# Units of two independently placed 128-row blocks in a routed feed-forward stage

## The reference

```
x = x + tanh(g_xattn) * xattn(layernorm(x), ctx)
logits = layernorm(x) @ gate_w          # 4096 tokens x 8 experts
topv, topi = top_k(logits, 2);  w = softmax(topv)
u = h @ Wu[e];  v = h @ Wv[e];  s = silu(u) * v;  Y = s @ Wo[e]     # 512 -> 128 -> 512
x = x + tanh(g_ffn) * sum over the two chosen experts of w * Y
```

## Time and profile before

| | us |
|---|---|
| median of 3 runs (lowest, highest) | 1020.25 (1018.52, 1021.1) |
| the profiled execution, its own time | 1017.04 |
| its span | 1015.3 |
| TensorE busy | 882.5 |
| VectorE busy | 689.9 |
| ScalarE busy | 568.1 |
| GpSimd busy | 530.5 |
| mean granted TensorE clock | 0.96 |

### The profile page before, as it was taken

The page is one execution under the profiler, slowest core; times in us unless marked ns, Lnnn a source line. Parts: engine busy times, 40 slices in busy tenths (PEclk is TensorE's granted clock), DMA queues, the critical chain, the costliest instruction groups (busy, mean ns, idle before and its releaser), DMA issues. The chain is left out here.

```text
span 1015.3 us, 22868 instructions
## 1 busy us (share of the span) xinstructions
PE 882.5 (87%) x8250; PEld 536.1 (53%) x8250; DVE 689.9 (68%) x1612; ACT 568.1 (56%) x1022; POOL 530.5 (52%) x643
## 2 busy tenths in 40 slices
PE   4878999999999999999999999997670899899990
PEld 2334555555555555555555555554340678677770
DVE  5577987677877887787787688688466455345540
ACT  4367766567546656755666665566430466456550
POOL 6222253454466456546545654547754155667765
PEclk9999999999999999999999999999885899999995
DMA  7557834645652354355245433753423589899997
GB/s 264 144 152 225 266 119 123 187 118 116 162 158 73 102 166 109 79 157 164 64 118 151 111 77 95 246 180 95 151 95 136 157 183 206 169 215 213 221 170 100
DMA packets 120509, 153.21 MB, mean 151 GB/s; under 512 B 42960, under 2 KB 75728, under 8 KB 119632
## 3 DMA queue, kind: packets, MB, share of 16 engines
q1 hardware_dynamic: 96624, 101.77, 35.2%
q0 software_dynamic: 16864, 37.40, 18.8%
q10 hardware_dynamic: 6912, 12.59, 4.1%
HBM read 67.06 MB, written 56.56 MB: 122 GB/s over the span
## 5 line engine op out<-in xcount | busy, mean ns | idle before, releaser
L700 POOL TENSOR_TENSOR Pl<-P,Ph 128x512 f16<-128x512 f32 x128 | 152.6, 1203 | 167.5 <-ACT Ph L786 167.0
L783 ACT ACTIVATE P<-ST 128x512 f32<-128x512 f32 x256 | 154.5, 603 | 128.9 <-PE ST L1476 109.2
L984 DVE TENSOR_REDUCE mx<-MX 128x1 f32<-128x512 f32 x256 | 168.7, 685 | 27.9 <-PE MX L1461 27.6
L786 ACT ACTIVATE Ph<-ST 128x512 f16<-128x512 f32 x256 | 155.7, 608 | 1.2 <-remote 0.7
L750 POOL DMA_INDIRECT out_dram<-V,Ph x78 | 121.9, 1563 | 62.2 <-ACT V L938 43.7
L1678 PE MATMUL MX<-heads,tiles 128*128 128x256 f16 x936 | 116.8, 276 | 5.7 <-DVE heads L1359 5.4
L1488 PE MATMUL PV<-V,Ph 128*128 128x65 f16 x1024 | 112.0, 194 | 9.8 <-issue 9.6
L1490 PE MATMUL PV<-V,Ph 128*128 128x64 f16 x1024 | 112.2, 195 | 1.8 <-issue 1.8
L1492 PE MATMUL PV<-V,Pl 128*128 128x65 f16 x1024 | 111.8, 193 | 0.7 <-issue 0.6
L1488 PEld LDWEIGHTS PV<-V,Ph 128*128 128x128 f16 x1024 | 96.4, 97 | 29.8 <-issue 11.8
L1490 PEld LDWEIGHTS PV<-V,Ph 128*128 128x128 f16 x1024 | 95.9, 98 | 19.1 <-issue 1.8
(11 more groups left out here) (261 smaller groups left out, 1880.1 us busy)
## 6 DMA issues: line engine op xcount, KB each, us to landing
heads<-expert_rows SPq DMA_DIRECT2D x39, 516.0 KB
heads<-q_hi SPq DMA_DIRECT2D x124, 64.0 KB, 2.5
heads<-k_hi SPq DMA_DIRECT2D x124, 64.0 KB, 2.9
second_norm<-in_x_dram SPq DMA_DIRECT2D x28, 256.0 KB, 3.1
out_dram<-second_norm SPq DMA_DIRECT2D x28, 256.0 KB, 2.2
tiles<-in_x_dram ACTq DMA_DIRECT2D x24, 256.0 KB, 3.1
tiles<-in_ctx_dram ACTq DMA_DIRECT2D x24, 256.0 KB, 3.9
expert_rows<-zero_rows SPq DMA_DIRECT2D x8, 516.0 KB, 5.6
```

What stands on the lines that cost most here:

```text
L700: nc.gpsimd.tensor_tensor(Pl[:, hh, c, :], P32[:, c, :], Ph[:, hh, c, :], ALU.subtract).then_inc(pl_pool, 1)
L783: nc.scalar.activation(P32[:, c, :], ST[:, c % 2, :], ACT.Exp, scale=0.125 / SC2).then_inc(p_ready, 1)
L786: nc.scalar.activation(Ph[:, hh, c, :], ST[:, c % 2, :], ACT.Exp, scale=0.125 / SC2).then_inc(ph_ready, 1)
L984: nc.vector.tensor_reduce(out=mx[:, k // TT, k % TT:k % TT + 1], in_=MX[:, (k + odd) % 2, :], axis=AXX, op=ALU.max).then_inc(mx_taken, 1)
```

## The change

A unit is now two blocks of 128 list rows, and each block (a "window") has its own expert, its own first row and its own flags. Lists are rounded up to multiples of 128: `WINDOWS = 64 + 8 = 72`, `UNITS = 36`.

- SyncE reads two offsets and issues two row loads per unit, one row to a partition in each.
- TensorE reads two experts per unit; `up` runs the 12 products once for each window, on 128 columns; `down` takes each window's weights.
- VectorE's table runs over 72 windows; the last window of a list now comes fourth; two bounds (`EARLY = (3, 4)`); flags between windows 1, 2 and 3 apart (`shared`).
- GpSimd issues the two adds one by one, each behind a count from the table and a `hold`. In the first two units the second add waits for the first.
- Blank prefixes and outsiders: half as many rows, 4 and 8 DMAs where there were 8 and 16.
- Scale selection (`unit_weights`) has one more small instruction.

```diff
-    UR = 2 * P
-    REGION = UR + ROWS
-    UNITS = ROWS * K // UR + E - 1
+    UR = K * P
+    REGION = P + ROWS
+    WINDOWS = ROWS * K // P + E
+    UNITS = WINDOWS // K
-    EARLY = 3
+    EARLY = (3, 4)
...
-                first = sp.value_load(unit_off[0:1, s:s + 1], min_val=0, max_val=E * REGION - UR)
-                sp.dma_start(xg_words[:, r], table[bass.ds(first, UR), :].rearrange("(p k) c -> p k c", k=K)) \
-                    .then_inc(rows_ld[r], 16)
+                for k in range(K):
+                    w = s * K + k
+                    first = sp.value_load(unit_off[0:1, w:w + 1], min_val=0, max_val=E * REGION - P)
+                    sp.dma_start(xg_words[:, r, k], table[bass.ds(first, P), :]).then_inc(rows_ld[r], 16)
...
-                for t in range(K):
-                    nc.gpsimd.indirect_dma_start(table.rearrange("r (q w) -> (r q) w", w=4),
-                                                 bass.IndirectOffsetOnAxis(out_pos[:, t, e:e + 1], 0),
-                                                 out_head[:, t, :].bitcast(U32), None).then_inc(outsider_st, 16)
+                nc.gpsimd.indirect_dma_start(table.rearrange("r (q w) -> (r q) w", w=4),
+                                             bass.IndirectOffsetOnAxis(out_pos[:, e:e + 1], 0),
+                                             out_head[:].bitcast(U32), None).then_inc(outsider_st, 16)
...
                 hold()
-                pool.wait_ge(y_taken, K * (s + 1))
+                pool.wait_ge(y_taken, K * s + 1)
                 since(pool, added[s % 2], s // 2 * 2 * 16)
-                for k in range(K):
-                    nc.gpsimd.indirect_dma_start(out_rows, bass.IndirectOffsetOnAxis(ids[:, s, k:k + 1], 0),
-                                                 y_sb[:, s % YR, k, :], None, compute_op=ALU.add) \
-                        .then_inc(added[s % 2], 16)
+                add(s, 0)
+                if s < 2:
+                    pool.wait_ge(added[s % 2], 16)
+                else:
+                    first = pool.value_load(need[1][0:1, s:s + 1], min_val=2 * 16, max_val=32 * UNITS)
+                    pool.wait_ge(added[s % 2], first)
+                hold()
+                pool.wait_ge(y_taken, K * s + 2)
+                add(s, 1)
...
+                for k in range(len(EARLY)):
+                    link(nc.vector.tensor_tensor(ucmp2, ucmp, spread_e(nt[:, 2 + k, :]), ALU.mult))
+                    link(nc.vector.tensor_reduce(before, ucmp2, AXX, ALU.add))
+                    nc.vector.tensor_tensor(late[k], limit, before, ALU.is_ge)
+                    link(nc.vector.scalar_tensor_tensor(out=early[k], in0=limit, scalar=float(P), in1=before,
+                                                        op0=ALU.add, op1=ALU.is_le))
+
+                def shared(dst, d):
+
+                    here, there = slice(d, WINDOWS), slice(0, WINDOWS - d)
+                    dst, apart, differ = dst[:, here], other[:, here], flag[:, here]
+                    nc.vector.tensor_tensor(differ, ue[:, here], ue[:, there], ALU.not_equal)
+                    nc.vector.tensor_tensor(apart, late[0][:, there], early[0][:, here], ALU.mult)
+                    link(nc.vector.tensor_tensor(dst, late[1][:, there], early[1][:, here], ALU.mult))
+                    link(nc.vector.tensor_tensor(apart, apart, dst, ALU.max))
+                    link(nc.vector.tensor_tensor(dst, off[:, here], off[:, there], ALU.subtract))
+                    nc.vector.scalar_tensor_tensor(out=differ, in0=apart, scalar=0.5, in1=differ, op0=ALU.is_lt, op1=ALU.mult)
+                    link(nc.vector.tensor_tensor(dst, dst, dst, ALU.mult))
+                    link(nc.vector.scalar_tensor_tensor(out=dst, in0=dst, scalar=float(P * P), in1=differ,
+                                                        op0=ALU.is_lt, op1=ALU.max))
...
-                for k, (m, a, c) in enumerate(parts):
-                    w = FW[n][m][:, bass.ds(e, 1), c * P:(c + 1) * P].rearrange("p o n -> p (o n)")
-                    last = nc.tensor.matmul(dst, w, uT[:, s % 2, a, c * UR:(c + 1) * UR], start=k == 0,
-                                            stop=k == len(parts) - 1)
+                for t in range(K):
+                    for k, (m, a, c) in enumerate(parts):
+                        w = FW[n][m][:, bass.ds(e[t], 1), c * P:(c + 1) * P].rearrange("p o n -> p (o n)")
+                        last = nc.tensor.matmul(dst[:, t * P:(t + 1) * P], w,
+                                                uT[:, s % 2, a, c * UR + t * P:c * UR + (t + 1) * P], start=k == 0,
+                                                stop=k == len(parts) - 1)
...
-                        w = FW["o"][m][:, bass.ds(e, 1), :].rearrange("p o n -> p (o n)")
+                        w = FW["o"][m][:, bass.ds(e[t], 1), :].rearrange("p o n -> p (o n)")
...
-            def expert_of(s):
-                return pe.value_load(unit_expert[0:1, s:s + 1], min_val=0, max_val=E - 1)
+            def experts_of(s):
+                return [pe.value_load(unit_expert[0:1, w:w + 1], min_val=0, max_val=E - 1)
+                        for w in range(K * s, K * s + K)]
```

More of the change, by code:

```diff
@@ L1142, in unit_table @@
             def unit_table():
-                spread_e = lambda z: z.unsqueeze(1).to_broadcast([P, UNITS, E])
-                spread_u = lambda z: z.unsqueeze(2).to_broadcast([P, UNITS, E])
-                before, block_, limit, off, over, blocks, flag, bound, early = (uw[:, k, :] for k in range(9))
+                spread_e = lambda z: z.unsqueeze(1).to_broadcast([P, WINDOWS, E])
+                spread_u = lambda z: z.unsqueeze(2).to_broadcast([P, WINDOWS, E])
+                before, block_, limit, off, over, blocks, flag, other = (uw[:, k, :] for k in range(8))
@@ L1151, in unit_table @@
+                late, early = ([uw[:, 8 + 2 * i + k, :] for k in range(2)] for i in range(2))
                 link(nc.vector.tensor_tensor(nt[:, 0, :], base[:], C["start"][:], ALU.subtract))
-                nc.vector.tensor_scalar(nt[:, 1, :], nt[:, 0, :], float(-UR), None, ALU.add)
-                nc.vector.tensor_tensor(nt[:, 2, :], early_base[:], C["start"][:], ALU.subtract)
+                nc.vector.tensor_scalar(nt[:, 1, :], nt[:, 0, :], float(-P), None, ALU.add)
+                for k in range(len(EARLY)):
+                    nc.vector.tensor_tensor(nt[:, 2 + k, :], early_base[:, k, :], C["start"][:], ALU.subtract)
@@ L1174, in unit_table @@
                 link(nc.vector.tensor_tensor(ucmp2, ucmp, spread_e(nt[:, 1, :]), ALU.mult))
-                link(nc.vector.scalar_tensor_tensor(out=blocks, in0=blocks, scalar=-2.0, in1=flag,
+                link(nc.vector.scalar_tensor_tensor(out=blocks, in0=blocks, scalar=-4.0, in1=flag,
                                                     op0=ALU.add, op1=ALU.mult))
@@ L1195, in unit_table @@
-                link(nc.vector.tensor_reduce(bound, ucmp2, AXX, ALU.add))
-                link(nc.vector.scalar_tensor_tensor(out=early, in0=limit, scalar=float(UR), in1=bound,
-                                                    op0=ALU.add, op1=ALU.is_le))
-                link(nc.vector.tensor_tensor(bound, limit, bound, ALU.is_ge))
-                link(nc.vector.tensor_tensor(bound[:, 0:UNITS - 1], bound[:, 0:UNITS - 1], early[:, 1:UNITS], ALU.mult))
-                link(nc.vector.tensor_tensor(before[:, 0:UNITS - 1], ue[:, 1:UNITS], ue[:, 0:UNITS - 1], ALU.not_equal))
@@ L1206, in unit_table @@
-                link(nc.vector.tensor_tensor(step_, step_, before[:, 0:UNITS - 1], ALU.max))
-                nc.vector.scalar_tensor_tensor(out=need[:, 1:UNITS], in0=step_, scalar=32.0, in1=C["need"][:, 0:UNITS - 1],
-                                               op0=ALU.mult, op1=ALU.add).then_inc(need_ready, 1)
+                nc.vector.tensor_tensor(valid.rearrange("p u k -> p (u k)"), C["row_no"][:].to_broadcast([P, WINDOWS]),
+                                        block_, ALU.is_ge)
+                for k in range(len(EARLY)):
+                    link(nc.vector.tensor_tensor(ucmp2, ucmp, spread_e(nt[:, 2 + k, :]), ALU.mult))
[3 more added lines that the diff above has]
+                                                        op0=ALU.add, op1=ALU.is_le))
@@ new lines, in unit_table @@
+                one, two, three = before, block_, blocks
+                for d, dst in ((1, one), (2, two), (3, three)):
+                    shared(dst, d)
+                of = lambda z, k: z.rearrange("p (u k) -> p u k", k=K)[:, 1:UNITS, k:k + 1].rearrange("p u o -> p (u o)")
+                flags = other[:, 0:UNITS - 1], other[:, UNITS:2 * UNITS - 1]
+                nc.vector.tensor_tensor(flags[0], of(one, 0), of(two, 0), ALU.max)
+                link(nc.vector.tensor_tensor(flags[1], of(two, 1), of(three, 1), ALU.max))
@@ new lines, in unit_table @@
+                link(nc.vector.tensor_tensor(flags[0], flags[0], flags[1], ALU.max))
```

(7 more changed lines are left out.)

126 lines of the change are left out of this document (58 added, 68 removed).

## The result

The kernel after takes 1049.34 us, median of 4 runs (1048.35 to 1052.79), against 1020.1 (1018.52 to 1021.1) for the kernel before on the same chip: ratio 1.0294, 95% interval 1.0267 to 1.0321. It is slower by 29 us, as forecast (1049, range 1030 to 1067).

What follows compares the result with a forecast made beforehand. The prediction took TensorE's array (4.81 us a unit) as the bound, then its sequencer (6.5) after the change. Span 796.2 + 234 + 1 + 3 + 10.2 = 1044.4; median 1020.25 + 29 = 1049 us, range 1030 to 1067.

Steps and rivals of the forecast that it cites:

- The mechanism: Units' stage: the change makes TensorE's sequencer the bound, 6.5 us a unit against 4.87 for the array.
- The first rival (the sequencer does not bind): Units' stage: sequencer steps shrink or run beside the issue, about 5.3 us a unit, 1006 us; chance 0.11.
- The pace of the sequencer: TensorE's sequencer, per unit: addresses 4.46 us, two expert readings 1.60, waits and transposes 0.4; sum 6.5 us.
- 36 x 0.124: TensorE's sequencer, per unit: 36 register instructions where there were 18, at 0.124 us each, 4.46 us.
- The array busy about three quarters: TensorE's array in the units' stage: a sign of the prediction being right, idle a quarter of the time.
- Attention: "nothing, at most a microsecond of gain": GpSimd in attention: 8 outsiders' DMAs of 1.02 us less and half the blank rows gain nothing, at most a microsecond.
- The table: VectorE before the first unit: a longer table puts the first up-matmul at 796.2 instead of 792.69, 3.5 us.
- The end: From TensorE's end to GpSimd's last add: 3 us, before 13.9; then 10.2 us to the span's end stay.
- GpSimd and DMA: Units' stage: GpSimd busy some 5 us a unit, costing nothing; row loads in 2064-byte packets 4.9 to 6.5, nearer 4.9.
- The clock: TensorE in the units' stage: expected at 1.00; the rival, half clock, 104 us more, 1153 us, chance 0.04.
- The sum: Whole span: start 796.2, units 234, half clock 1, end 3 and 10.2: 1044.4, which is 29.1 over 1015.3.

Runs made afterwards that it cites:

- c_two: Kernel before with the change's TensorE code: two expert readings, `up` in 128-column halves, own addresses for each half, `down` too; ratio 1.0602.
- l_down: Kernel after with `down` taking the first window's expert for both, 34 addresses a unit instead of 36; 1043.64 us, ratio 1.0227 to the kernel before.
- m_onev: Kernel after with v computed with the first window's expert for both windows, 28 addresses a unit; 1020.39 us, ratio 0.9995 to the kernel before.
- l_third: Kernel after with a third, unused expert reading per unit on TensorE; 1070.81 us, ratio 1.0492 to the kernel before.
- h_wide: Kernel after with TensorE's part as before: one expert reading, `up` on 256 columns, `down` with one expert; ratio 0.9899 to the kernel before.
- c_split: Kernel before with each up-matmul of 256 columns cut in two of 128, both halves with the same expert and addresses; ratio 1.0018.
- e_outs: Kernel before with 8 outsiders' DMAs instead of 16; ratio 0.9970.
- g_even: Kernel before with all 16 outsiders' DMAs, two in the first and third step of each batch of four (before: first and second); ratio 1.0002.

## Why the prediction held, and where it did not

**The mechanism** held. c_two shows it alone: two expert registers, with their readings and their addresses and everything else as before, make the kernel slower, and l_down, m_onev and l_third show that addresses and readings each count. The first rival (the sequencer does not bind) and its 5.3 us a unit is what h_wide measures, and the kernel after is not there.

**The pace of the sequencer** was 6.5 us a unit, and is 6.71. From the starts of TensorE's sequencer instructions over 27 units: 36 addresses at 0.132 us are 4.76 (forecast 36 x 0.124 = 4.46); two readings 1.54 (forecast 1.60); three waits 0.42 (forecast 0.4): 6.72. The step that was mis-sized is "36 x 0.124": 0.124 is the median, and some 12% of the steps take 0.15 to 0.31. I used the mean for the loads and the median for the steps.

**The array busy about three quarters** failed as a sign, though its cause held: the rows show 213.07 of 243 us. A matmul's row is 0.22 us long and the next may start 0.06 after it, so gaps of up to 0.16 us don't show. c_split shows 40.00 of 40.00 with a unit in 4.87, this kernel 35 of 40 with one in 6.7: a busy share says little of pace where short matmuls are handed over one by one. The better sign was the same 24 matmuls taking 1.50 us from the queue and 2.21 at the sequencer's pace.

**Attention: "nothing, at most a microsecond of gain"** is the step that failed. It was 4.3 us between the two traces. One pair of traces is a weak measure of it, since the same attention of the kernel after reaches the table's first large operation between 770.40 and 775.40 us in four traces (after, l_down, l_third, m_onev); the medians of e_outs give 3.8 us for the same DMAs. I took GpSimd's idle time as slack for every placement of its work; its products collide with VectorE's in four steps.

**The table** took 2.7 us more from its first large operation to the first up-matmul (21.06 against 18.32), and 0.3 ahead of it: 3.0, forecast 3.5. Part of that is an addition: 4 x 0.78, 20 x 0.27 and 13 x 0.13 are 10.2 us and not 10.8, which would have made the forecast 2.9.

**The end** was costed at 3 us from TensorE's end to the last add, and took 4.7 (1033.0 to 1037.74): the second add of the unit before last still had to go out ahead of the last two, at 1.95 us each.

**GpSimd and DMA** held. The first adds wait for one another (804.08, 810.30, 815.93, 821.20, 827.02) and no stall reaches TensorE; `hold` waits 22.4 us for landings in the whole stage: twice at the start (809.85, 820.86) and for three flagged units (865.87, 880.28, 947.14), as many as the lists had said. Row loads between 841 and 861:

```profile
q1 hardware_dynamic: 867, 1.59, 24.9%
```

That is 15.7% per MB against 14.4: packets of half the size cost a tenth more per byte, near the end that was taken and far from double.

**The clock** held: 1.00 from 794.8 to 1037, with TensorE idle for 0.46 to 1.08 us ahead of nearly every up u. The Trainium skill, page "TensorE: Matmul & The Clock Gate", section "A second HAM failure mode: psum-queue depth-cycling", tells of another kernel in which frequent micro-idles between matmul groups made the clock oscillate. Here they did not.

**The sum**: start 4.7 us early (attention 4.3, table 0.4), units 6.5 late, end 1.7 late, so the span came out 3.5 above its 1044.4. That the median met 1049 to half a microsecond is luck: errors of 4.7, 6.5 and 1.7 us nearly cancel, and the 3.5 that is left was made good because the profiled execution of before was 3.2 below its median and that of after was not.

Not tried: pairing the windows so that all units but the few at the lists' ends have one expert and one set of addresses. It might reach toward h_wide's 0.9899 with the whole computation, but needs another table and other flags.

## What to carry to other kernels

Where matmuls take their weights by a register, count the different addresses that the engine's sequencer works out (0.13 us each here) and the register readings (0.77 each), and compare the sum with the array's time: two registers where there was one doubled it here, and matmuls of half the width did not matter. Idle time of GpSimd is slack only where its operations don't meet those of VectorE that wait for them; look for VectorE rows far above the shortest of their kind, and move work into the idle time ahead of a wait, not behind it.

## What the runs showed of the hardware beyond that

- Forty-eight matmuls of 128 columns take a unit no longer, within the measurement, than twenty-four of 256: 1.0018 (c_split).
- An operation of 32 columns and 0.18 us on VectorE stretched to nearly 2.9 us (two of them 2.98, g_even) beside two back-to-back GpSimd products of 2.28.
- Not only operations of two inputs stretch. A copy of two words a partition from one tile, 0.16 us otherwise, takes 1.13 us beside GpSimd's product in four steps of the kernel after (276, 364, 450 and 537 us) and in five of the kernel before. The kernel after:

```profile
363.76 1.13 DVE L1133 COPY second_norm<-idf 128x2 f32<-128x2 f32 x1
```

- The address of a weight slice, once worked out for an expert register, served the second half of an `up` at no cost: 624 register instructions with 1872 matmuls.
